# A graph network's x1·adj product made by seven block products in place of eight, from the third batch on

## The chip, the cores and the metric

The kernel runs on one core of one Trainium2 chip. The metric is device time in microseconds of one execution. The kernel before takes 539.05 us (median of three runs, 538.93 to 540.27).

## The reference, cut to what matters

Sixteen batches, each with node features `x` (512 x 256) and its own matrix `adj` (512 x 512), pass through four graph layers and two layer norms, all in float32:

```
num = adj.sum(axis=-1, keepdims=True)
x1 = layernorm(x + (adj @ (x @ W0 + b0)) / num)
a  = relu(adj @ (x1 @ W1) + b1)
b  = relu(adj @ (a @ W2) + b2)
out = layernorm(x1 + adj @ (b @ W3) + b3)
```

## The kernel before, in words

Every batch is cut into T = 4 tiles of 128 nodes and KF = 2 halves of 128 features. To keep float32 precision on TensorE, each operand is held as a pair: `hi`, a copy rounded to float32r, and `lo`, the rest. A product is then three matmuls, hi·hi, hi·lo and lo·hi (`three_passes`, L184 to L188). ScalarE makes each `hi` (`copy_hi`, L487, or a relu, L586), VectorE the matching `lo` by a subtraction (`sub_hi`, L694). For the inputs adj and xT the `lo` comes from GpSimd (L984, L991).

The products of a batch are numbered in the code. p0 is x·W0, its result h; p1 is adj·h, from which the first norm (`norm1`) makes x1; p2 is x1·adj in transposed form, its result g (256 features by 512 nodes); p3 is g·W1 (x2), p4 x2·W2 (s2), p5 s2·adj (x3), p6 x3·W3 (s3), p7 adj·s3, followed by the second norm (`norm2`) and the store.

The main loop overlaps three batches. `step(new)` works at `old` (one batch earlier) and `nxt` (one later). TensorE's queue in a step is p5(old), p2(new), p6(old), p3(new), p7(old), p0(nxt), p4(new), p1(nxt). p2 and p5 use moving tiles of 512 columns, all others 256. One step runs for each of the batches 1 to 14; the last batch has a tail of its own. Each engine executes its own queue in the order written in its `step`, and engines wait for one another by semaphores:

- ScalarE: relu of x3 (two halves, each once to `hi` and once in place in PSUM), g, split of xT(nxt), s3, x2, then `norm2(old)` with a row sum of adj beside each tile, h(nxt), s2(new), `norm1(nxt)` with the split of the batch after next's adj tiles.
- VectorE: the `lo` parts in the same order, `norm2`, h, s2, `norm1`. In `norm2` tile j's order is v2 (L840), then for tile j-1 the reciprocal, then `bn_stats` (L847), the normalization y of tile j-1 (a tensor_scalar, L853), and `bn_aggr` (L859); ScalarE answers each `bn_aggr` with a square root (L607). `norm1` has the same shape (L793 to L817), with the tensor_scalar at L804.
- GpSimd: waits until x1 is fully split (L997), then adj_lo (4 instructions), xT_lo (2), x + b0 (4), x1 + b3 (4).
- SyncE: one queue, in order: adjT of a batch in two halves (waits `adj_split`), xT, x, adj, then the store of an earlier batch, which waits for that batch's last y. The next batch's adjT stands behind that store.

PSUM is eight banks: `bank_a[0:4]` and `bank_b[0:4]`. v1, s3 and v2 use the left half of `bank_b`; x3 and x2 use `bank_a[0:2]`, g uses `bank_a[2:4]`.

Of the kernel before, what the change touches and what calls it, by code (L numbers as in the profile page):

```python
# [10 lines left out]
P = 128  # L11
# [8 lines left out]
def build(nc, xT, x, adjT, adj, w0, w123, b03, b12, out):  # L20
# [8 lines left out]
    with ExitStack() as ctx:  # L29
# [29 lines left out]


# [4 lines left out]
        g_hi, g_lo = pair("g", [P, KF, N])  # L65
        x2_hi, x2_lo = pair("x2", [P, KF, N])
        x3_hi, x3_lo = pair("x3", [P, KF, N])
# [10 lines left out]
        y = sb("y", [P, T, F], F32)  # L78
# [47 lines left out]
        p2_done = sem("p2_done")  # L126
        p3_done = sem("p3_done")
# [43 lines left out]
        def out_of(batch):  # L171

            return v1 if batch is LAST else y
# [19 lines left out]
        xT1_raw, x1_raw = y, v2  # L193
# [19 lines left out]
        def _(sp):  # L213
# [38 lines left out]
            sp.dma_start(out[0], y[:, :, :]).then_inc(stored, DMA)  # L252
            with sp.Fori(3, NB) as i:
                load(i, lambda half: sp.wait_ge(adj_split, (i - 3) * T + (half + 1) * T // 2),
                     lambda: sp.wait_ge(rows_ready, i * T))

                sp.wait_ge(y_ready, (i - 1) * T)
                sp.dma_start(out[i - 2], y[:, :, :]).then_inc(stored, DMA)
            sp.wait_ge(y_ready, (NB - 1) * T)
            sp.dma_start(out[NB - 2], y[:, :, :]).then_inc(stored, DMA)  # L260

            for j in range(T):
                sp.wait_ge(y_ready, (NB - 1) * T + j + 1)
                sp.dma_start(out[NB - 1, :, j, :], out_of(LAST)[:, j, :]).then_inc(stored, DMA)
# [3 lines left out]
        def _(pe):  # L268
# [114 lines left out]
            def p3(new):  # L383

                pe.wait_ge(g_split, at(new, KF, KF))
                for f in range(KF):
                    cols = slice(f * P, (f + 1) * P)

                    for side in (slice(0, N // 2), slice(N // 2, N)):
                        for k in range(KF):  # L390
                            mm = three_passes(pe, bank_x2(new)[f][:, side],
                                              (w_hi[:, 1, k, cols], w_lo[:, 1, k, cols]),
                                              (g_hi[:, k, side], g_lo[:, k, side]), k == 0, k == KF - 1)
# [11 lines left out]
            def p6(old, reader, read):  # L405
# [31 lines left out]
            def step(new):  # L437
                old, nxt = before(new), before(new, -1)
                p5(old)
                p2(new)  # L440
                p6(old, v1_ready, new)
                p3(new)
# [22 lines left out]
            with pe.Fori(0, TURNS - 1) as turn:  # L465
# [7 lines left out]
            p2(LAST)  # L473
            p6(old, v1_ready, LAST)
            p3(LAST)
# [9 lines left out]
        def _(act):  # L485
# [55 lines left out]

            def s3(old):
                hi = s3_last_hi if old is LAST else s3_hi
                for j in range(T):
                    if j == 0 and old is not LAST:
                        act.wait_ge(p6_done, at(old, T, 1))
                        act.activation(s3_half[:, :], bank_b[0][:, F:2 * F], ACT.Copy).then_inc(s3_second_half, 1)
# [21 lines left out]

            def norm1(new, ahead, turns=range(T + 1)):  # L570
# [8 lines left out]

            def g(new, f):  # L580
                act.wait_ge(p2_done, at(new, KF, f + 1))
                copy_hi(g_hi[:, f, :], bank_g(new)[f][:, :]).then_inc(g_hi_ready, 1)

            def relu_split(done, batch, f, bank, bias, hi, ready):
                act.wait_ge(done, at(batch, KF, f + 1))
                act.activation(hi[:, f, :], bank[:, :], ACT.Relu, bias=bias[:, f:f + 1])  # L586

                act.activation(bank[:, :], bank[:, :], ACT.Relu,  # L588
                               bias=bias[:, f:f + 1]).then_inc(ready, 1)

# [6 lines left out]
            def x3(old, f):  # L597
# [3 lines left out]
                relu_split(p5_done, old, f, bank_a[f], b2_col, x3_hi, x3_hi_ready)  # L601

            def norm2(old, tiles=range(T), nxt=None):

                for j in tiles:
# [3 lines left out]
                    if nxt is not None:  # L609
                        row_sum(nxt, j)  # L610

            def step(new, last=False, ahead=True):
                old, nxt = before(new), before(new, -1)
                x3(old, 0)
                x3(old, 1)
                g(new, 0)
# [3 lines left out]
                g(new, 1)  # L620
# [3 lines left out]
                if not last:  # L624
                    norm2(old, nxt=nxt)
                    h(nxt)
                    s2(new)
                    norm1(nxt, before(new, -2) if ahead else None)
# [48 lines left out]
            with act.Fori(0, TURNS - 1) as turn:  # L677
# [6 lines left out]
            x3(LAST, 0)  # L684
            x3(LAST, 1)
            norm2(before(LAST), range(2, 3))
# [5 lines left out]
        def _(dve):  # L692
# [88 lines left out]
            def norm1(new):  # L781

                for j in range(T + 2):
                    a, b, c = j, j - 1, j - 2
                    if a == 0:
# [33 lines left out]
            def g(new, f):  # L819
                dve.wait_ge(g_hi_ready, at(new, KF, f + 1))  # L820
                sub_hi(g_lo[:, f, :], bank_g(new)[f][:, :], g_hi[:, f, :]).then_inc(g_split, 1)
# [9 lines left out]
            def norm2(old, turns=range(T + 1), banks=bank_b):  # L831

                for j in turns:
                    a, b = j, j - 1
                    if a == 0:

                        dve.wait_ge(x1b_ready, at(old, T, T))
                    if a < T:
                        dve.wait_ge(p7_done, at(old, T, a + 1))
                        dve.tensor_tensor(v2[:, a, :], banks[a][:, 0:F], x1b[:, slot(old), a, :],  # L840
# [4 lines left out]
                    if a < T:  # L845
                        dve.wait_ge(v2_ready, at(old, T, a + 1))
                        dve.bn_stats(stats2[:, a, :], v2[:, a, :]).then_inc(stats2_ready, 1)  # L847
                    if b >= 0:
                        if b == 0 and old is not LAST:

                            dve.wait_ge(stored, at(old, DMA, DMA))
                        dve.wait_ge(rstd2_ready, at(old, T, b + 1))
                        dve.tensor_scalar(out_of(old)[:, b, :], v2[:, b, :], moments2[:, b, 0:1], rstd2[:, b:b + 1],  # L853
# [7 lines left out]
            def step(new, last=False):  # L861
                old, nxt = before(new), before(new, -1)
                x3(old, 0)
                x3(old, 1)
                g(new, 0)
                g(new, 1)
# [3 lines left out]
                if not last:  # L870
                    norm2(old)
                    h(nxt)
                    s2(new)
                    norm1(nxt)
# [187 lines left out]
```

## Time and profile before

| | |
|---|---|
| median of three runs | 539.05 us |
| the profiled execution | 539.36 us, span 537.6 us |
| granted TensorE clock | 0.998 of full speed |
| TensorE busy | 530.4 us, 3829 matmuls |
| VectorE busy | 351.2 us (65%) |
| ScalarE busy | 313.6 us (58%) |
| GpSimd busy | 208.3 us (39%) |
| one step of the main loop | 32.7 us |

The span is from the first to the last instruction; about 1.8 us of the execution's own time lies around it. Busy shares are averages over the whole span. Recorded durations of matmuls overlap, because the engine is pipelined: the distance between the starts of two matmuls is what one costs.

### The profile page before, as it was taken

The numbers are of one execution on the slowest core, as the hardware profiler recorded it, in microseconds if no ns is written. First come the engines' busy times: TensorE is split into PE (matmuls) and PEld (weight loads), VectorE is DVE, ScalarE is ACT, GpSimd is POOL, SyncE is SP. The second block draws the span as 40 slices with busy tenths as digits, with TensorE's granted clock in tenths as the row PEclk, the third lists the DMA queues.
The fourth block names the chain that finished last, engine by engine and source line by source line (L and its number), as shares of the span: only waits on it lengthen the run. The fifth ranks groups of instructions, "written<-read, shape, count | busy, mean of one in ns | idle before, by whom it ended". The sixth has DMA issues, their size and how long they took to land.

```text
span 537.6 us, 11046 instructions
## 1 busy us (share of the span) xinstructions
PE 530.4 (99%) x3829; PEld 497.0 (92%) x3829; DVE 351.2 (65%) x1061; ACT 313.6 (58%) x790; POOL 208.3 (39%) x225
## 2 busy tenths in 40 slices
PE   8999999999999999999999999999999999999996
PEld 7899989999899998989999899998999989899896
DVE  4884756747576575766747567475675757667546
ACT  5856566565665556655475665656655566554542
POOL 3749045090541807227081450905418062271100
PEclk9999999999999999999999999999999999999999
DMA  8530430705216060250703407042060612500002
GB/s 322 207 119 1 122 153 1 275 2 177 96 39 234 0 237 37 63 210 0 273 0 99 174 0 273 0 166 107 31 242 0 233 41 62 215 1 39 2 1 78
DMA packets 14566, 58.23 MB, mean 108 GB/s; under 512 B 1744, under 2 KB 2256, under 8 KB 12752
## 3 DMA queue, kind: packets, MB, share of 16 engines
q1 hardware_dynamic: 13824, 55.58, 28.3%
q10 hardware_dynamic: 720, 2.36, 1.2%
q8 instruction: 13, 0.21, 0.2%
q14 instruction: 9, 0.07, 0.0%
HBM read 49.55 MB, written 8.39 MB: 108 GB/s over the span
## 4 chain that ended last, share of the span: by engine, by line
PE 94%; DVE 2%; ACT 1%; issue 1%; DMA 1%; POOL 1%; POOLq 0%; DVEq 0%; SPq 0%
PE bank_a L186 16%; PE bank_a L187 16%; PE bank_a L188 16%; PE bank_b L186 15%; PE bank_b L188 15%; PE bank_b L187 15%; PE bank_b L278 1%; DMA xT_raw<-in_xT 1%; PE bank_b L279 1%; ACT x L565 0%; DVE stats L847 0%; ACT std L607 0%; ACT x_hi L567 0%; PE bank_b L314 0%; POOL w_both L954 0%
## 5 line engine op out<-in xcount | busy, mean ns | idle before, releaser
L984 POOL TENSOR_TENSOR adj_lo<-adj_raw,adj_hi 128x512 fp32r<-128x512 f32 x56 | 70.9, 1297 | 261.7 <-ACT adj_hi L487 261.7
L694 DVE TENSOR_TENSOR x_lo<-bank_a,x_hi 128x512 fp32r<-128x512 f32 x62 | 42.9, 692 | 66.9 <-ACT bank_a L588 66.9
L186 PE MATMUL bank_b<-h_hi,adj_hi 128*128 128x256 f32 (+1 forms) x256 | 71.1, 278 | 0.7 <-issue 0.5
L188 PE MATMUL bank_b<-h_hi,adj_lo 128*128 128x256 f32 (+1 forms) x256 | 70.8, 277 | 0.0
L187 PE MATMUL bank_b<-h_lo,adj_hi 128*128 128x256 f32 (+1 forms) x256 | 70.8, 277 | 0.0
L555 ACT ACTIVATE std<-moments,eps_col 128x1 f32<-128x1 f32 x64 | 18.9, 295 | 84.9 <-DVE moments L817 82.0
L188 PE MATMUL bank_b<-s_hi,adj_lo 128*128 128x256 f32 x232 | 64.1, 276 | 0.0
L186 PE MATMUL bank_b<-s_hi,adj_hi 128*128 128x256 f32 x232 | 64.0, 276 | 0.0
L187 PE MATMUL bank_b<-s_lo,adj_hi 128*128 128x256 f32 x232 | 64.0, 276 | 0.0
L586 ACT ACTIVATE x_hi<-bank_a,b_col 128x512 fp32r<-128x512 f32 x62 | 42.4, 684 | 20.6 <-PE bank_a L188 19.5
L949 POOL TENSOR_TENSOR x1b<-x,b_all 128x256 f32<-128x256 f32 x64 | 46.2, 748 | 17.2 <-DVE x L804 17.2
L186 PE MATMUL bank_a<-adj_hi,s_hi 128*128 128x512 f32 x128 | 50.1, 391 | 0.0
L187 PE MATMUL bank_a<-adj_lo,s_hi 128*128 128x512 f32 x128 | 50.0, 390 | 0.0
L188 PE MATMUL bank_a<-adj_hi,s_lo 128*128 128x512 f32 x128 | 49.8, 389 | 0.0
L607 ACT ACTIVATE std<-moments,eps_col 128x1 f32<-128x1 f32 x64 | 18.9, 295 | 51.9 <-DVE moments L859 51.9
L186 PEld LDWEIGHTS bank_b<-h_hi,adj_hi 128*128 128x128 f32 x256 | 48.1, 188 | 1.0 <-issue 1.0
L187 PEld LDWEIGHTS bank_b<-h_lo,adj_hi 128*128 128x128 f32 x256 | 48.1, 188 | 0.0
L188 PEld LDWEIGHTS bank_b<-h_hi,adj_lo 128*128 128x128 f32 x256 | 48.1, 188 | 0.0
L694 DVE TENSOR_TENSOR g_lo<-bank_a,g_hi 128x512 fp32r<-128x512 f32 x30 | 20.8, 692 | 40.0 <-ACT g_hi L487 40.0
L186 PE MATMUL bank_a<-adj_hi,x_hi 128*128 128x512 f32 x120 | 46.7, 389 | 0.0
L187 PE MATMUL bank_a<-adj_lo,x_hi 128*128 128x512 f32 x120 | 46.7, 389 | 0.0
L188 PE MATMUL bank_a<-adj_hi,x_lo 128*128 128x512 f32 x120 | 46.7, 389 | 0.0
(154 smaller groups left out, 1719.4 us busy)
## 6 DMA issues: line engine op xcount, KB each, us to landing
adj_raw<-in_adjT SPq DMA_DIRECT2D x29, 512.0 KB, 5.4
adj_rows<-in_adj SPq DMA_DIRECT2D x14, 1024.0 KB, 9.2
xT_raw<-in_xT SPq DMA_DIRECT2D x15, 512.0 KB, 6.4
out_y<-y SPq DMA_DIRECT2D x15, 512.0 KB, 2.9
x_raw<-in_x SPq DMA_DIRECT2D x14, 512.0 KB, 7.2
w_raw<-in_w SPq DMA_DIRECT2D x1, 768.0 KB, 13.4
adj_raw<-in_adjT ACTq DMA_DIRECT2D x1, 512.0 KB, 6.1
x_raw<-in_x ACTq DMA_DIRECT2D x1, 512.0 KB, 8.1
```

The source lines that it names most:

```text
L186: pe.matmul(acc, st[0], mv[0], start=start, stop=False)
L187: pe.matmul(acc, st[0], mv[1], start=False, stop=False)
L188: return pe.matmul(acc, st[1], mv[0], start=False, stop=stop)
L278: pe.matmul(bank[j][:, 0:2 * F], hi, w_both[:, n, k, :, :], start=True, stop=False)
L279: mm = pe.matmul(bank[j][:, 0:F], lo, mv[0], start=False, stop=False)
L555: act.activation(std1[:, j:j + 1], moments1[:, j, 1:2], ACT.Sqrt, bias=eps_col[:, :]).then_inc(std1_ready, 1)
L586: act.activation(hi[:, f, :], bank[:, :], ACT.Relu, bias=bias[:, f:f + 1])
L607: act.activation(std2[:, j:j + 1], moments2[:, j, 1:2], ACT.Sqrt, bias=eps_col[:, :]).then_inc(std2_ready, 1)
L694: return dve.tensor_tensor(lo, full, hi.bitcast(F32), ALU.subtract)
L949: pool.tensor_tensor(x1b[:, slot(batch), j, :], x1[:, j, :], b3_all[:, :], ALU.add).then_inc(x1b_ready, 1)
L984: pool.tensor_tensor(adj_lo[:, s, k, :], adj_raw[:, k, :], adj_hi[:, s, k, :].bitcast(F32), ALU.subtract).then_inc(adj_split, 1)
```

## The change

p2 for the batches 2 to 15 is computed by a Winograd-Strassen scheme. x1 is seen as 2 x 2 blocks (two tiles of nodes by 128 features), adj as 2 x 2 blocks (two tiles by 256 columns). Seven products m1 to m7 of such blocks take the place of eight: each is two tiles x three passes = six matmuls of 256 columns, written to half banks of PSUM. Four of the seven need sums of x1 blocks (S1 to S4, VectorE), and four need sums of adj blocks (T1 to T4, GpSimd), and each sum is again split in `hi` (ScalarE) and `lo` (VectorE for S, GpSimd for T). VectorE then combines the products: c11 = m1 + m2, u = m6 + m1, w = m7 + u, v = m5 + u, c21 = m4 + w, c22 = m7 + v, c12 = m3 + v. Batch 1 keeps the old form.

Further edits come with it. ScalarE's g follows the combinations, with both halves after them; `split_xT` moves behind g; `row_sum` of the last tile moves behind h; one `split_adj` tile moves from `norm1` into the next step. GpSimd's step gets four sums T after adj_lo and four T_lo at its end, and starts when all S are split. The store now reads v2, which is normalized in place. VectorE does the last y of `norm2` after h. SyncE's load of adjT waits for the four sums T in place of `adj_split`. x3 shares its buffer with x2, g with h, the sums T live in the buffer of the raw weights, and m1's copy, u, v and w live in `xb`. The first turn of the loop is written out.

```diff
+            def p2_by_seven(new):
...
+                pe.wait_ge(x1_split, at(new, T, 2))
+                product(m1, x1_block(0, low), adj_block(low, left)).then_inc(m1_done, 1)
+                pe.wait_ge(x1_split, at(new, T, T))
+                product(m2, x1_block(0, high), adj_block(high, left)).then_inc(m2_done, 1)
+                pe.wait_ge(T_split, at(new, 4, 4 - 8))
+                pe.wait_ge(S_split, at(new, 4, 1 - 8))
+                product(m7, S_block(S3), T_block(T3))
+                product(m4, x1_block(1, high), T_block(T4))
+                pe.wait_ge(S_split, at(new, 4, 3 - 8))
+                product(m6, S_block(S2), T_block(T2)).then_inc(m6_done, 1)
+                product(m5, S_block(S1), T_block(T1)).then_inc(m5_done, 1)
+                pe.wait_ge(S_split, at(new, 4, 4 - 8))
+                pe.wait_ge(c11_added, at(new, 1, -1))
+                product(m3, S_block(S4), adj_block(high, right)).then_inc(m3_done, 1)
...
             def p6: ready(j):
+                    if by_seven and j > 0:
+                        pe.wait_ge((u_ready, v_ready, m1_copied)[j - 1], at(read, 1, -1))
...
         ScalarE:
             def step(new, last=False, ahead=True, by_seven=True):
                 x3(old, 0)
+                    split_S(new, S1)
+                x3_in_place(0)
+                    split_S(new, S2)
+                    copy_m1(new)
+                    split_S(new, S4)
                 x3(old, 1)
+                x3_in_place(1)
+                        split_adj(nxt, T - 1)
+                    g_by_seven(new)
+                s3_halved(old)
                     split_xT(nxt, 0)
                     split_xT(nxt, 1)
                 s3(old)
                 x2(new, 0)
                 x2(new, 1)
+                    for i in range(4):
+                        split_T(nxt, i)
                     norm2(old, nxt=nxt)
                     h(nxt)
+                    row_sum(nxt, T - 1)
                     s2(new)
+                    norm1_and_S(nxt, before(new, -2) if ahead else None)
...
         VectorE:
             def step(new, last=False, by_seven=True):
+                    sum_S(new, S2)
+                    sum_S(new, S4)
+                    split_S(new, S1)
+                    x3(old, 0)
+                    split_S(new, S2)
+                    add_c11(new)
+                    split_S(new, S4)
+                    x3(old, 1)
+                    add_u(new)
+                    add_w(new)
+                    add_v(new)
+                    add_c21(new)
+                    add_c22(new)
+                    add_c12(new)
+                    g(new, 1, 0)
+                    g(new, 0, 1)
                 s3(old)
                 x2(new, 0)
                 x2(new, 1)
+                    norm2(old, range(0, T))
                     h(nxt)
+                    norm2(old, range(T, T + 1))
                     s2(new)
+                    norm1(nxt, first_sums=not by_seven)
...
         GpSimd:
             def step(new, by_seven=True):
+                    pool.wait_ge(S_split, at(new, 4, 4 - 8))
                 split_adj(nxt)
+                sum_T(nxt)
                 split_xT(nxt)
                 add_b0(nxt)
                 add_b3(new)
+                split_T(nxt)
```

`sum_S(S3)` and `sum_S(S1)` with `split_S(S3)` stand in VectorE's last two turns of `norm1`, the copy of S3 in ScalarE's. `sum_T` is four subtractions of 128x512 elements, `split_T` four more; on ScalarE `split_T` is one 128x512 copy each.

## Rows read from the trace of the kernel before

**Rows 1.** The page: busy times, granted clock by slice, shares of the last chain

```profile
PE 530.4 (99%) x3829; PEld 497.0 (92%) x3829; DVE 351.2 (65%) x1061; ACT 313.6 (58%) x790; POOL 208.3 (39%) x225
PEclk9999999999999999999999999999999999999999
PE 94%; DVE 2%; ACT 1%; issue 1%; DMA 1%; POOL 1%; POOLq 0%; DVEq 0%; SPq 0%
```

**Rows 2.** Timeline, TensorE: start us, duration, instruction; where p2, p6, p7, p0 begin

```profile
205.38 0.39 PE L186 MATMUL bank_a<-adj_hi,x_hi 128*128 128x512 f32 x1
...
210.82 0.40 PE L278 MATMUL bank_b<-w_both,x_hi 128*128 128x512 f32 x1
...
216.27 0.28 PE L186 MATMUL bank_b<-s_hi,adj_hi 128*128 128x256 f32 x1
...
221.71 0.39 PE L278 MATMUL bank_b<-w_both,xT_hi 128*128 128x512 f32 x1
```

**Rows 3.** Timeline, SyncE: store, load, next store; from the page, adjT's time to landing

```profile
224.44 0.36 SPq L258 DMA_DIRECT2D out_y<-y  x1
225.35 0.91 SPq L234 DMA_DIRECT2D adj_raw<-in_adjT  x2
...
257.12 0.36 SPq L258 DMA_DIRECT2D out_y<-y  x1
...
adj_raw<-in_adjT SPq DMA_DIRECT2D x29, 512.0 KB, 5.4
```

**Rows 4.** Timeline, ScalarE, one step; [idle before it <- who released it]

```profile
204.37 0.42 ACT L487 ACTIVATE x_hi<-x 128x256 fp32r<-128x256 f32 x1
204.69 0.62 ACT L487 ACTIVATE adj_hi<-adj_raw 128x512 fp32r<-128x512 f32 x1
205.21 0.67 ACT L586 ACTIVATE x_hi<-bank_a,b_col 128x512 fp32r<-128x512 f32 x1
205.78 0.65 ACT L588 ACTIVATE bank_a<-bank_a,b_col 128x512 f32<-128x512 f32 x1
...
219.55 0.29 ACT L607 ACTIVATE std<-moments,eps_col 128x1 f32<-128x1 f32 x1 [1.84 <-DVE moments L859]
...
224.13 0.36 ACT L531 ACTIVATE h_half<-bank_b 128x256 f32<-128x256 f32 x1
224.99 1.21 ACT L487 ACTIVATE h_hi<-bank_b 128x256 fp32r<-128x256 f32 x4 [0.50 <-DVE bank_b L720]
```

**Rows 5.** Timeline, VectorE, the same step

```profile
217.74 0.69 DVE L694 TENSOR_TENSOR x_lo<-bank_a,x_hi 128x512 fp32r<-128x512 f32 x1 [0.61 <-ACT bank_a L588]
218.35 0.41 DVE L840 TENSOR_TENSOR v<-bank_b,x1b 128x256 f32<-128x256 f32 x1
218.80 0.43 DVE L847 BATCH_NORM_STATS2 stats<-v 128x6 f32<-128x256 f32 x1
...
228.72 0.48 DVE L798 SCALAR_TENSOR_TENSOR v<-bank_b,inv_rows,xb 128x256 f32<-128x256 f32 x1 [0.43 <-PE bank_b L188]
...
236.61 0.42 DVE L804 TENSOR_SCALAR x<-v,moments,rstd 128x256 f32<-128x256 f32 x1
```

**Rows 6.** Timeline, GpSimd in the step: its first, second and last pieces

```profile
205.40 5.06 POOL L984 TENSOR_TENSOR adj_lo<-adj_raw,adj_hi 128x512 fp32r<-128x512 f32 x4 [19.45 <-ACT adj_hi L487]
210.43 2.58 POOL L991 TENSOR_TENSOR xT_lo<-xT_raw,xT_hi 128x512 fp32r<-128x512 f32 x2
...
215.79 2.85 POOL L949 TENSOR_TENSOR x1b<-x,b_all 128x256 f32<-128x256 f32 x4
```

**Rows 7.** Timeline of the start, GpSimd

```profile
32.29 0.72 POOL L949 TENSOR_TENSOR x1b<-x,b_all 128x256 f32<-128x256 f32 x1
```

**Rows 8.** Timeline of the start, VectorE beside it

```profile
27.80 1.81 DVE L694 TENSOR_TENSOR w_both<-w_raw,w_both 128x512 fp32r<-128x512 f32 x1
...
32.32 0.84 DVE L766 TENSOR_SCALAR x<-v,moments,rstd 128x256 f32<-128x256 f32 x1
33.09 0.41 DVE L770 BATCH_NORM_STATS2 stats<-v 128x6 f32<-128x256 f32 x1
```

More of the change, by code:

```diff
@@ L58, in build @@
         s2_hi, s2_lo = pair("s2", [P, T, F])
+        S_hi, S_lo = pair("S", [P, 4, 2, P])
         inv_rows = sb("inv_rows", [P, T], F32)
@@ L64, in build @@
         xT_hi, xT_lo = pair("xT", [P, T, F])
-        g_hi, g_lo = pair("g", [P, KF, N])
+        T_hi, T_lo = pair("T", [P, 4, 2, N // 2])
         x2_hi, x2_lo = pair("x2", [P, KF, N])
-        x3_hi, x3_lo = pair("x3", [P, KF, N])
+        x3_hi, x3_lo = x2_hi, x2_lo
         s3_hi, s3_lo = pair("s3", [P, T, F])
@@ L191, in build, with rows_of, g_of @@
         adj1_raw = adj_rows
-        xT1_raw, x1_raw = y, v2
+        xT1_raw, x1_raw = v2, S_raw.rearrange("p a b c -> p a (b c)")
+        T_raw = w_raw
+        S3, S1, S2, S4 = range(4)
+        T1, T3, T2, T4 = range(4)
+        def rows_of(t, width):
+            return t.rearrange("p a b -> p (a b)")[:, 0:KF * width].rearrange("p (k n) -> p k n", k=KF)
+        def g_of(batch):
+            hi, lo = (s3_hi, s3_lo) if batch is FIRST else (h_hi, h_lo)
+            return rows_of(hi, N), rows_of(lo, N)
+        left, right = slice(0, N // 2), slice(N // 2, N)
+        c11, c12 = bank_a[2][:, left], bank_a[2][:, right]
+        c21, c22 = bank_a[3][:, left], bank_a[3][:, right]
+        m2, m3, m4, m7 = c11, c12, c21, c22
+        m6, m5, m1 = [bank_b[j][:, right] for j in range(1, T)]
+        m1_copy, u, v, w = [xb[:, j, :] for j in range(T)]
         def bank_g(batch):
@@ L464, in _ @@
             pe.wait_ge(w123_split[2], 1)
-            with pe.Fori(0, TURNS - 1) as turn:
+            for r in range(1, RING + 1):
+                step((0, r), by_seven=r > 1)
+            with pe.Fori(1, TURNS - 1) as turn:
                 for r in range(1, RING + 1):
@@ L676, in _ @@
             norm1(second, third, range(2, T + 1))
-            with act.Fori(0, TURNS - 1) as turn:
+            for r in range(1, RING + 1):
+                step((0, r), by_seven=r > 1)
+            with act.Fori(1, TURNS - 1) as turn:
                 for r in range(1, RING + 1):
@@ L913, in _ @@
             norm1_early(second, range(3, T + 2))
-            with dve.Fori(0, TURNS - 1) as turn:
+            for r in range(1, RING + 1):
+                step((0, r), by_seven=r > 1)
+            with dve.Fori(1, TURNS - 1) as turn:
                 for r in range(1, RING + 1):
@@ L1020, in _ @@
                 add_b3(FIRST, range(j, j + 1))
-            with pool.Fori(0, TURNS - 1) as turn:
+            pool.wait_ge(w0_split, 1)
+            pool.wait_ge(w123_split[2], 1)
+            for r in range(1, RING + 1):
+                step((0, r), by_seven=r > 1)
+            with pool.Fori(1, TURNS - 1) as turn:
                 for r in range(1, RING + 1):
```

246 lines of the change are left out of this document (196 added, 50 removed).

## The prediction, made before the changed kernel ran

> **What bounds the kernel now.** I read the page first: TensorE is 99% busy, its clock stands at the upper level (2.4 GHz, granted 9 or more tenths in all slices), and 94% of the last chain is TensorE's [rows 1]. Then its timeline. p2's 24 matmuls of 512 columns run from 205.38 to 210.82, so one costs 5.44/24 = 0.227 us; p7's 48 of 256 columns from 216.27 to 221.71, 0.1133 us each [rows 2]. There is no gap between products: TensorE waits for nothing. A step takes 257.12 - 224.44 = 32.68 us [rows 3]. Last I read the other queues of one step, since the question is how much room they leave.
>
> **What p2 saves.** 42 matmuls of 256 columns x 0.1133 = 4.76 us in place of 5.44: 0.68 us a batch, 14 batches, 9.5 us. The price per column is the same at both widths [rows 2], and p7 too changes its weights at every matmul, so more weight changes cost nothing by themselves. If nothing else were late: 539.36 - 9.5 = 529.8 us by the profiled execution, a step of 32.0.
>
> **The chain of the helpers.** ScalarE and VectorE hand work to each other in a circle: norm1, x3, g, s3, x2, norm2, h, s2, norm1. Now it closes with room only because TensorE feeds it: v1 waits 0.43 us for TensorE at 228.72 [rows 5]. I follow the circle in the changed queues from A, the start of v1 of tile 0, using distances between starts, TensorE taken as ready.
> - A to x1 of tile 3: 236.61 - 228.72 = 7.89 [rows 5]. ScalarE's copy of tile 3 would follow 0.45 later (8.34), but S3's copy stands before it: 8.65 (a 256 copy costs 204.69 - 204.37 = 0.32, [rows 4]).
> - From there ScalarE has no pause: x1, x3 (0.57), S1, x3 in place, S2, m1's copy (0.27), S4, x3, x3 in place. The 256 copies cost 0.31, each relu 205.78 - 205.21 = 0.57 [rows 4]. The last one starts at 11.88, and VectorE follows 0.68 later: 12.56.
> - VectorE: x3_lo 218.35 - 217.74 = 0.61, then u, w, v, c21, c22, c12 at some 0.34 to 0.45 each (a dependent one costs 218.80 - 218.35 = 0.45, [rows 5]). c12 starts at 15.0. ScalarE's two g copies: 15.10 and 15.59, then s3's half 16.08 and the two of xT: 17.39. s3's four copies (as h's, 1.21 for four, [rows 4]) end at 18.56, s3_lo at 19.3.
> - x2's four relus: 2.28, to 20.84. Then four copies of T (0.53 each), the last not before GpSimd's T4. GpSimd starts when S4 is split, 12.4; adj_lo takes 5.06 [rows 6] and the four T, of the same form, as much: 22.5. The T4 copy ends at 23.13, where norm2's first root starts; without T it could start at 22.76.
> - Three tiles of norm2 at 1.25 (219.55 to the fourth root, three turns, and 0.2 to h_half at 224.13 less the row sum that moves away): h_half at 27.1, h_hi at +0.86 = 27.95 [rows 4]. Four copies to 29.04, row sum 0.61, s2's four; VectorE, which has h_lo, the last y and s2_lo in between, reaches v1 of the next batch at 31.84.
>
> So the circle needs 31.84, against TensorE's 32.0. There is one more term: the last y now comes after h, at 30.3, some 2.5 us later in its step than before, and adjT's load stands behind the store in SyncE's queue. It is issued 0.19 + 0.91 later, 31.4, and lands 5.4 after that [rows 3], 36.8; ScalarE wants it at A + 3.70 = 35.54. The wait eats its own pause before the next root (A + 5.24) and 0.16 remains, between 0 and 0.4. Everything is balanced to a few tenths: 32.0.
>
> **What I did not find room for.** GpSimd has 14 instructions a step now and 22 after, some 23.4 us: from A + 12.4 to about A + 36, that is to 4 us into the next norm1. Now it is done at 218.6, before the first y (two turns after v2 at 218.35), and does not start until norm1 is over [rows 6], so no y or x1 of the main loop ever meets it. After, all four y and x1 of tile 0 do. What such a meeting costs the trace shows once: the tensor_scalar of x1 issued at 32.32 took 0.84 us, and what followed it started 0.77 later, where the loop's duration of 0.42 [rows 5] leaves 0.32 to the next; GpSimd's add, begun at 32.29, ended at 33.01 [rows 7, 8]. That looks like waiting for the whole instruction of GpSimd. A subtraction with both inputs in SBUF, of a form that costs 0.69 where it has one in PSUM, took 1.81 in the same stretch [rows 8].
> So a tensor_scalar costs what is left of GpSimd's instruction, less 0.24. For y of tile 0: T4's end releases ScalarE's copy (0.53), the root (0.33 to the reciprocal), 0.08, 0.32: y is issued about 1.32 after T4's end. GpSimd begins its second xT_lo 1.23 after it. y comes just behind it and loses 0.96. y of tiles 1 and 2 meet the adds of 0.71: 0.3 each. The last y meets an add or a T_lo, its place less certain: 0.41, the mean over a 1.26 instruction. x1 of tile 0 falls near the end of T_lo: nothing. Sum 1.96, bounds 0 (below nothing is excluded, a meeting gives nothing back) and 2 x 1.02 + 2 x 0.47 = 3.0. VectorE's other work of that stretch has one input in PSUM, as x_lo and v2 at 217.74 and 218.35 have, which keep 0.69 and 0.41 while GpSimd adds until 218.6 [rows 5, 6]; I cost it at nothing. S's sums and S_lo, with both inputs in SBUF, fall between T_lo's end and GpSimd's start, by its new wait.
>
> The Trainium skill, SBUF — State Buffer, section Who interferes with whom, states this rule: VectorE and GpSimd share a pair of ports, an instruction in the two-port mode (a float32 tensor_scalar from SBUF to SBUF may be in it) takes the pair for its whole length, and the one that comes second is blocked. The row at 32.32 agrees, with 0.84. By the rule the sum is the one above; if it did not hold, the sum ends at the circle of 32.0.
>
> **The sum.** A step of 31.84 + 0.16 + 1.96 = 33.96 against 32.68: +1.28, for 13 steps 16.6; the last batch keeps its 0.68. 539.36 + 16.6 - 0.7 = 555.3 by the profiled execution, 0.3 above the median of the runs: 555.0. TensorE then waits about 2 us a step, first for h_lo (before p1) and v2, then for the splits of x3 and g.
>
> **Rivals.**
> - *The queues just fit* (the other side). The meeting costs next to nothing, and the step is 32.0 to 32.2, with TensorE pausing 0.1 to 0.2 at g (its last split ends at A + 17.0, which is 13.4 us into the step; p3 wants it at 13.3). For it: the circle as worked out. Against: the 0.84. It gives 539.36 - 14 x 0.68 + 13 x 0.1 = 531; 532 with the store's delay. It decides when the meetings cost under 0.7 us a step.
> - *y slips in front.* y of tile 0 is 0.1 us behind the start of xT_lo; a tenth earlier it waits for the instruction before, which is nearly over. Then y costs 0.2 in all, but T_lo ends later into norm1 and x1 of tile 0 pays up to 0.55: a step of 32.8, 13 x 0.1 - 0.7: 540.
> - *All at the worst phase*: 3.0 in place of 1.96 and 0.4 for the load: 35.2, 572.
>
> **Chances.** Forecast 0.50 (its own range 545 to 565), queues just fit 0.31, since one row carries the whole price against it, y in front 0.15, worst phase 0.04. A measurement of this kernel can tell 0.3% from no change, 1.6 us. Faster: 0.31 and a third of 0.15, 0.36. Same: a third of 0.15 and the edge of the forecast's spread, 0.08. Slower: 0.56. The range that holds 8 in 10 reaches down to the case that fits: 531 to 563.
>
> **What would show it.** Right: y of norm2 much longer than 0.40 us, over 1 us for tile 0; a step of 33 to 34.5; TensorE idle before p1 and p3; GpSimd busy from p6 to beyond the next step's start. Wrong: y at 0.40 us beside a busy GpSimd; or a step near 32.0 with v1 again waiting for TensorE. If p2 itself is not 4.76 us, the first term is wrong.

## The result, and the profile after

The changed kernel takes 572.2 us (median; 570.1 to 581.2) against 539.2 (538.9 to 540.3): ratio 1.061, interval 1.059 to 1.063. It is slower, as forecast, but by 33 us and not by 16, above the range (531 to 563). The profiled execution is the slowest of the five, 581.2; where its extra 9 us lie is said below. One execution each of runs 7 and 13, over 1.5% above their others (644.7 and 586.0 us), is left out of their times.

The page of the changed kernel: busy times, granted clock by slice, the last chain, and y's group (its mean was 0.40 us in the kernel before).

```profile
PE 547.2 (94%) x4081; PEld 521.2 (90%) x4081; DVE 457.4 (79%) x1271; ACT 356.2 (61%) x916; POOL 351.4 (61%) x337
PEclk9999799999999999999999999769999999999999
PE 31%; DVE 24%; issue 15%; ACT 13%; POOL 8%; DMA 7%; SPq 1%; DVEq 0%; POOLq 0%
L1065 DVE TENSOR_SCALAR v<-v,moments,rstd 128x256 f32<-128x256 f32 x64 | 65.3, 1020 | 0.6
```

TensorE's share of the last chain fell from 94% to 31% [rows 1]; the 64 instructions y take 1.02 us in the mean. SyncE's stores (the columns as in [rows 3]) give the step:

```profile
206.68 0.36 SPq L299 DMA_DIRECT2D out_y<-v  x1
...
240.91 0.36 SPq L299 DMA_DIRECT2D out_y<-v  x1
```

Of the 13 steps between two stores nine take 33.9 to 34.2 us, where 33.96 was forecast; two take 34.7 and 35.3, and two, at 240.91 and 346.08, 37.0 and 46.6. In one of the ordinary steps VectorE's four y and, in the second fence, GpSimd beside them:

```profile
96.19 1.39 DVE L1065 TENSOR_SCALAR v<-v,moments,rstd 128x256 f32<-128x256 f32 x1
98.44 0.61 DVE L1065 TENSOR_SCALAR v<-v,moments,rstd 128x256 f32<-128x256 f32 x1
99.91 0.61 DVE L1065 TENSOR_SCALAR v<-v,moments,rstd 128x256 f32<-128x256 f32 x1
103.65 0.98 DVE L1065 TENSOR_SCALAR v<-v,moments,rstd 128x256 f32<-128x256 f32 x1
```

```profile
94.86 2.58 POOL L1224 TENSOR_TENSOR xT_lo<-xT_raw,xT_hi 128x512 fp32r<-128x512 f32 x2
97.37 3.00 POOL L1176 TENSOR_TENSOR xb<-x_raw,b_all 128x256 f32<-128x256 f32 x4
100.33 2.90 POOL L1182 TENSOR_TENSOR x1b<-x,b_all 128x256 f32<-128x256 f32 x4
103.18 2.61 POOL L1247 TENSOR_TENSOR T_lo<-w_raw,T_hi 128x512 fp32r<-128x512 f32 x2
```

Over 0.40 they lose 0.99, 0.21, 0.21 and 0.58: 1.99 a step, where 1.96 was forecast. The first y ends at 97.58, as GpSimd's second xT_lo does (97.44). The next two meet adds that start 0.72 apart, and the last a T_lo. So far each y ends 0.15 after the one instruction of GpSimd that it met. Two y of the 64 did not: first VectorE, then GpSimd.

```profile
56.51 7.54 DVE L1065 TENSOR_SCALAR v<-v,moments,rstd 128x256 f32<-128x256 f32 x1
...
377.07 9.38 DVE L1065 TENSOR_SCALAR v<-v,moments,rstd 128x256 f32<-128x256 f32 x1
```

```profile
58.95 4.95 POOL L1247 TENSOR_TENSOR T_lo<-w_raw,T_hi 128x512 fp32r<-128x512 f32 x4
...
381.36 4.93 POOL L1247 TENSOR_TENSOR T_lo<-w_raw,T_hi 128x512 fp32r<-128x512 f32 x4
```

The first ends at 64.05, the second at 386.45; the last T_lo end at 63.90 and 386.29. These y waited out the rest of GpSimd's unbroken run, eight and eleven instructions with the one under way. Two other pauses of some 3 us stand where a turn of the loops ends (VectorE, then TensorE behind it):

```profile
254.88 0.43 DVE L950 TENSOR_TENSOR S_raw<-S_raw,x 128x256 f32<-128x256 f32 x1 [2.96 <-issue]
```

```profile
257.09 0.39 PE L204 MATMUL bank_b<-T_hi,S_hi 128*128 128x256 f32 x1 [2.71 <-DVE S_lo L848]
```

"issue" says that VectorE waited for nothing that the profile shows. The other pause ends at 360.19 and is 3.10 us long. TensorE then stood idle for 2.9 us, and its granted clock fell to 0.50 (the lower level, 1.2 GHz) from 364 to 368. The wait of 9.38 came in the same step, TensorE idle for 7.1 in p0 and the granted clock again at 0.50 from 388 to 392: the step took 46.6 us. Less the pause, which the other turn's end has too, that is 9.5 us over an ordinary step, about what the profiled execution has over the median (9.0). Whether the other executions had such a wait is not known.

TensorE in the changed kernel, where p2, p6, p7 and p0 begin (as [rows 2]):

```profile
216.74 0.28 PE L204 MATMUL bank_b<-adj_hi,x_hi 128*128 128x256 f32 x1
...
222.38 0.40 PE L319 MATMUL bank_b<-w_both,x_hi 128*128 128x512 f32 x1
...
228.04 0.28 PE L204 MATMUL bank_b<-s_hi,adj_hi 128*128 128x256 f32 x1
...
233.69 0.39 PE L319 MATMUL bank_b<-w_both,xT_hi 128*128 128x512 f32 x1
```

p7's 48 products, which the change did not touch, take 233.69 - 228.04 = 5.65 us; before, 5.44 [rows 2]. This row did not decide the time of this kernel (run 13), but what the change can give at most (runs 6, 9 and 14).

### The profile page after: what moved, and what is told of

Read it like the earlier page. It is cut to its first block, busy times and chain, and to the rows that moved or that the text cites. A ratio compares the mean times of both kernels' runs of the same rounds, so it can differ in the third digit from the quotient of the medians.

```text
span 579.4 us, 12001 instructions
## 1 busy us (share of the span) xinstructions
PE 547.2 (94%) x4081; PEld 521.2 (90%) x4081; DVE 457.4 (79%) x1271; ACT 356.2 (61%) x916; POOL 351.4 (61%) x337
## 4 chain that ended last, share of the span: by engine, by line
PE 31%; DVE 24%; issue 15%; ACT 13%; POOL 8%; DMA 7%; SPq 1%; DVEq 0%; POOLq 0%
DMA adj_raw<-in_adjT 7%; PE bank_a L204 6%; PE bank_a L206 6%; PE bank_a L205 6%; PE bank_b L204 4%; PE bank_b L205 4%; PE bank_b L206 4%; POOL w_raw L1235 4%; ACT T_hi L577 4%; POOL adj_lo L1217 3%; DVE stats L1062 2%; DVE h_lo L848 2%; DVE v L1065 2%; ACT std L740 2%; DVE x L1015 2%
## 5 line engine op out<-in xcount | busy, mean ns | idle before, releaser
L204 PE MATMUL bank_b<-h_hi,adj_hi 128*128 128x256 f32 (+1 forms) x256 | 73.0, 285 | 4.4 <-DVE h_lo L848 4.1
L1247 POOL TENSOR_TENSOR T_lo<-w_raw,T_hi 128x512 fp32r<-128x512 f32 x56 | 71.5, 1307 | 0.0
L1065 DVE TENSOR_SCALAR v<-v,moments,rstd 128x256 f32<-128x256 f32 x64 | 65.3, 1020 | 0.6
L1182 POOL TENSOR_TENSOR x1b<-x,b_all 128x256 f32<-128x256 f32 x64 | 46.8, 758 | 4.9 <-DVE x L1015 4.9
L1176 POOL TENSOR_TENSOR xb<-x_raw,b_all 128x256 f32<-128x256 f32 x60 | 44.4, 770 | 0.0
L577 ACT ACTIVATE adj_hi<-adj_raw 128x512 fp32r<-128x512 f32 x60 | 37.5, 626 | 11.0 <-DMA adj_raw<-in_adjT 10.9
```

What stands on the lines that cost most here:

```text
L204: pe.matmul(acc, st[0], mv[0], start=start, stop=False)
L577: return act.activation(dst, src, ACT.Copy)
L1065: dve.tensor_scalar(v2_of(old)[:, b, :], v2_of(old)[:, b, :], moments2[:, b, 0:1], rstd2[:, b:b + 1], ALU.subtract, ALU.mult).then_inc(y_r ...
L1176: pool.tensor_tensor(xb[:, j, :], raw[:, j, :], b0_all[:, :], ALU.add).then_inc(xb_ready, 1)
L1182: pool.tensor_tensor(x1b[:, slot(batch), j, :], x1[:, j, :], b3_all[:, :], ALU.add).then_inc(x1b_ready, 1)
L1247: pool.tensor_tensor(T_lo[:, i, :, :], T_raw[:, i, :, :], T_hi[:, i, :, :].bitcast(F32), ALU.subtract).then_inc(T_split, 1)
```

## The experiments

Ratios are to the kernel before, with their 95% intervals. Theory A: what is lost is lost where y meets GpSimd. Its rival B: something else in the added work is late, and y only stands beside it.

**1. y without the two operands' arithmetic.** It leaves the normalization of y out.

```
-  dve.tensor_scalar(v2[:, b, :], v2[:, b, :], moments2[:, b, 0:1], rstd2[:, b:b + 1], subtract, mult)
+  dve.bn_stats(stats_dummy[:, b, :], v2[:, b, :])
```

> The changed kernel with the y instruction of the second norm (a tensor_scalar from SBUF to SBUF) replaced by a bn_stats of the same input, which takes 0.41 us as y does alone; the normalization of the output is left out. All waits and queues stay. Theory A (y meets GpSimd's instructions and waits for them, and for a whole run of them in the first step): the 1.98 us a step and the 7 us of the first step go, the step falls from 34.0 to 32.0-32.2 us, and the time to about 537, of which 6 us are two pauses of 3 us at the loop's ends. Theory B (the circle of ScalarE and VectorE is simply longer than worked out, whatever GpSimd does): the time stays within 5 us of 572.

557.2 us, 1.032 (1.031 to 1.034): 15 us come back, not 35. The long wait is gone, the first step (by p5's starts) is back from 39.9 to 32.7, and no bn_stats waits. But VectorE is now earlier, and x1 of tile 0, at 0.40 in the changed kernel, meets T_lo (VectorE, GpSimd):

```profile
133.38 1.53 DVE L1016 TENSOR_SCALAR x<-v,moments,rstd 128x256 f32<-128x256 f32 x1
```

```profile
132.15 2.62 POOL L1247 TENSOR_TENSOR T_lo<-w_raw,T_hi 128x512 fp32r<-128x512 f32 x2
```

1.1 us of the 2.0 that y gave back are lost there, up to 1.25 in other steps: the cost moved to the next tensor_scalar. The ordinary step is 33.5.

**2. y with a sum beside it.** The same instruction with an accumulated column, which does not apply the scale to each element (that part is left out).

```
+  ..., subtract, mult, junk[:, b:b + 1])
```

> The changed kernel with y as a tensor_scalar that also writes an accumulator (into a column nobody reads), everything else as it is. Theory A with the mode of the instruction as cause (it takes both ports only in its fast form): y takes 0.5 us beside GpSimd in every step, never over 1 us, no long wait; step 32.2-32.6 us, time 538 to 543. Rival A2 (any VectorE instruction from SBUF to SBUF of this kind waits for GpSimd, in whatever form): y stays at 1.4, 0.6, 0.6, 1.0 us and the time at 572. Theory B: 572 or a little more, with y at 0.5 us.

559.3 us, 1.036 (1.034 to 1.038). This form takes 0.52 to 0.54 us beside GpSimd in every step. So not every instruction of VectorE that reads v2 waits; its form decides. The time missed the 538 to 543 expected, as run 1 missed its 537: here too x1 of tile 0 takes 1.2 to 1.45.

**3. The loops written out** (`for turn in range(1, TURNS - 1)` in place of `Fori(1, TURNS - 1)`, on the four compute engines).

> The changed kernel with the loop over turns written out on all four engines. Theory C (two pauses of 3 us before VectorE's first sum of S, at the jump back to the loop's start): both go, and with them the fall of TensorE's clock that followed the second in the profiled run: time down by 6, to 565-567. Rival: the pause is the fetch of instructions as such and comes elsewhere or more often in a longer program: 570 or more.

567.4 us, 1.052 (1.050 to 1.054): 4.8 us less than the changed kernel, and the pauses of 3 us are gone. The steps stay at 33.9, the wait at 56.79 at 7.54 us. TensorE, where p5 begins in the second step and in the last batch:

```profile
77.06 0.39 PE L204 MATMUL bank_a<-adj_hi,s_hi 128*128 128x512 f32 x1
...
517.97 0.39 PE L204 MATMUL bank_a<-adj_hi,s_hi 128*128 128x512 f32 x1
```

The kernel before has the same kind of loop, and its turns' ends show no such pause. VectorE there, behind a turn's end and in a step without one:

```profile
141.09 0.69 DVE L694 TENSOR_TENSOR x_lo<-bank_a,x_hi 128x512 fp32r<-128x512 f32 x1 [1.22 <-ACT bank_a L588]
...
173.78 0.69 DVE L694 TENSOR_TENSOR x_lo<-bank_a,x_hi 128x512 fp32r<-128x512 f32 x1 [1.22 <-ACT bank_a L588]
```

In both VectorE stands idle for 1.22 us, waiting for ScalarE. A pause of up to 1.2 us could hide there, one of 3 could not. What makes a turn's end of the changed kernel cost that much stays open.

**4. The meeting by itself.** VectorE and GpSimd alone, one instruction of VectorE a trial against a row of GpSimd's adds, issued later from trial to trial.

> A kernel of its own, in which only VectorE and GpSimd work: GpSimd adds in runs of 14 (128x256, 0.71 us apart) or 10 (128x512, 1.26 us apart), and one VectorE instruction is issued after the fourth of them, later by 0.08 us from trial to trial. It computes nothing of the reference. Theory A: a tensor_scalar takes 0.15 us plus what is left of the GpSimd instruction; and, as the two long cases of the changed kernel (issued with 0.39 and 0.20 us left of an instruction) against the short ones (0.46 or more left), those issued in the last 0.4 us or so wait for the end of the whole run, 6 us and more. Rival A3 (the long wait has nothing to do with the moment of issue): no trial waits for a run, or it does at random. The tensor_tensor from SBUF behaves like the tensor_scalar, bn_stats stays at 0.41 throughout, and the tensor_scalar with an accumulator at 0.5 if its form decides.

443.2 us in all. VectorE's rows: against adds of 256 columns, the same five trials later, against adds of 512, and the form with a sum:

```profile
8.45 0.79 DVE L70 TENSOR_SCALAR vc<-va,one 128x256 f32<-128x256 f32 x1 [3.06 <-POOL pc L54]
...
57.44 0.47 DVE L70 TENSOR_SCALAR vc<-va,one 128x256 f32<-128x256 f32 x1
...
108.09 1.33 DVE L70 TENSOR_SCALAR vc<-va,one 128x256 f32<-128x256 f32 x1 [10.42 <-POOL pc L54]
...
376.02 0.52 DVE L72 TENSOR_SCALAR_CACHE_REDUCE vc<-va,one 128x256 f32<-128x256 f32 x1
```

Alone it takes 0.41. Issued 0.065 us later each time, it takes 0.065 less: a wait for the end of GpSimd's instruction, never beyond. A tensor_tensor waits in the same way (0.42 to 0.93), the form with a sum and bn_stats never. No moment of issue gave a long wait, so the moment alone does not make it.

**5. and 6. The same results without a meeting.** x1 and y as a scalar_tensor_tensor whose second operand is the reciprocal root, a column in PSUM read over and over; TensorE gets two waits, so that it does not clear the columns too soon. First with the loops, then with them written out.

```
-  dve.tensor_scalar(y, v2, mean, rstd2[:, b:b + 1], subtract, mult)
+  dve.scalar_tensor_tensor(y, v2, mean, rstd_psum[:, b:b + 1].broadcast_to([P, F]), subtract, mult)
```

> The changed kernel with y and x1 of the main loop's two norms as scalar_tensor_tensor, the reciprocal root read as a broadcast column from a free place in PSUM: the same result by an instruction that has one input in SBUF and one in PSUM, as v1's has, which takes 0.47 us in place of 0.40. TensorE gets two waits that should be satisfied already. Theory A (with y replaced alone, the step was 33.5 us, since x1 of tile 0 then met T_lo and took 1.5 to 1.65 us): no meeting is left in the loop, the step falls to the circle's own 32.0-32.3 plus 8 x 0.07, 32.5 to 32.9 us; time 540 to 545, of which 5 to 6 us are the two pauses at the loop's ends. Theory B (the circle itself is longer): the step stays at 33.3 or more, 550 or more.

> The same with the loop written out on the four engines. The pauses at the loop's ends go (they went in the changed kernel written out, which took 5 us less): 5 us below psum_all, 535 to 540. Rival: with shorter steps the pauses were partly hidden, and it is 2 us or less.

550.3 us, 1.021 (1.019 to 1.022), and written out 541.4, 1.004 (1.002 to 1.005). Against the runs of 572.2 and 567.4 the meetings cost 22 and 26 us. Both times are above what was expected (540 to 545, 535 to 540). Writing out gave 8.9 us in place of 5: the two steps with a turn's end take 35.3 and 37.1. y takes 0.46 to 0.48, beside GpSimd or not:

```profile
221.48 0.47 DVE L1081 SCALAR_TENSOR_TENSOR v<-v,moments,bank_a 128x256 f32<-128x256 f32 x1
```

But a step is 32.66, not the 32.0 that TensorE was to need (written out; five of the 13 take 32.8 to 33.1). At first I laid that to the circle of ScalarE and VectorE. The timeline of TensorE contradicts it (p2, p6, p7, p0, p1 begin):

```profile
206.60 0.28 PE L204 MATMUL bank_b<-adj_hi,x_hi 128*128 128x256 f32 x1
...
211.60 0.40 PE L319 MATMUL bank_b<-w_both,x_hi 128*128 128x512 f32 x1
...
217.26 0.28 PE L204 MATMUL bank_b<-s_hi,adj_hi 128*128 128x256 f32 x1
...
222.91 0.39 PE L319 MATMUL bank_b<-w_both,xT_hi 128*128 128x512 f32 x1
...
228.37 0.28 PE L204 MATMUL bank_b<-h_hi,adj_hi 128*128 128x256 f32 x1
```

No row of that step has idle time. p2 takes 5.00 (42 x 0.119), p6 with p3 5.66 and p7 5.65, that is 0.1177 a product; from p0 on it is 0.1133 again (5.46 for p0 with p4; before, 5.45). The clock is granted in full throughout.

**7. GpSimd's new work alone.** The kernel before, with four sums and four subtractions a step on GpSimd and the load of adjT behind them.

> The kernel before with GpSimd's new work alone: the four sums T and four instructions in the place of T_lo (T less itself, so that ScalarE has nothing to do with it), at the changed kernel's places in GpSimd's queue; the eight products and every other queue stay, the sums are not used. Theory A: y of the loop takes 0.6 to 1.4 us where it took 0.40, x1 of the first tiles may too; of 1 to 3 us a step about 0.4 has room, so the step is 33.2 to 34.5 and the time 546 to 565, more if y waits for a whole run of GpSimd. Theory B (GpSimd's work is harmless, the sums on the other engines cost): 539 to 541.

610.3 us, 1.132 (1.128 to 1.136), more than the whole change. The first y of two steps:

```profile
95.37 7.44 DVE L857 TENSOR_SCALAR y<-v,moments,rstd 128x256 f32<-128x256 f32 x1
...
216.83 0.65 DVE L857 TENSOR_SCALAR y<-v,moments,rstd 128x256 f32<-128x256 f32 x1
```

In 9 of 14 steps the first y of a step takes 6.7 to 7.5 us, in 5 it takes 0.65 to 0.82. A step with the long wait takes 39.7 to 40.8 us, one without it 33.4 to 34.4 (theory A's range was 33.2 to 34.5). The long wait is thus no accident of one step; it needs neither S nor the seven products. Theory A stands and theory B falls. Six of the long ones and four of the short ones begin 0.23 to 0.27 us into the same add of GpSimd, so the place does not decide.

**8. A run without a pause.** As 4, with bn_stats ahead of an in-place tensor_scalar, against eight adds and four subtractions in a row.

> A kernel of its own, nothing of the reference: GpSimd in runs as behind xT_lo (eight adds of 128x256, four subtractions of 128x512 into float32r), with and without satisfied waits ahead of each; VectorE issues bn_stats and right behind it an in-place tensor_scalar, later by 0.065 us from trial to trial. The first probe showed no wait beyond the instruction under way at any moment. If the long wait of 7.5 us comes from this order of instructions, some trials take 5 us or more; if not, all take 0.4 to 0.8, and the long wait needs something that is only in the whole kernel.

237.5 us in all; 0.40 to 0.90 in every trial, never a long wait. What makes VectorE wait for the rest of the run in the kernels stays open.

**9. p2 of the kernel before in halves.** 48 products of 256 columns in place of 24 of 512.

```
+  for side in (slice(0, N // 2), slice(N // 2, N)):
       for k in range(T):
-          three_passes(bank[f][:, :], x1[:, k, cols], adj[:, s, k, :])
+          three_passes(bank[f][:, side], x1[:, k, cols], adj[:, s, k, side])
```

> The kernel before, with its p2 alone written in products of 256 columns in place of 512 (48 in place of 24, the same columns of work; no S, no T, no new wait). It is to tell where TensorE's slower pace behind the seven products comes from: in the kernel before 256-column products stand 0.1133 us apart everywhere; in the changed kernel and in the one with the PSUM forms they stand 0.1177 to 0.1183 apart from p2's first product to the end of p7 (136 products, 0.60 us a batch), though no wait is seen there. Theory F (the form: a p2 of 256-column products has the slower pace and passes it on to p6, p3 and p7): p2 takes 5.65 in place of 5.44, the 94 products behind it 0.42 more, a batch 33.3, the whole 547 to 549. Theory W (the pace goes down where TensorE's queue meets a wait that is fulfilled just in time, and stays down): the pace stays at 0.1133, the whole within 0.3% of 539.3.

550.4 us, 1.019 (1.018 to 1.021). TensorE at p2, p6, p7, p0:

```profile
209.85 0.28 PE L186 MATMUL bank_a<-adj_hi,x_hi 128*128 128x256 f32 x1
...
215.60 0.40 PE L278 MATMUL bank_b<-w_both,x_hi 128*128 128x512 f32 x1
...
221.26 0.28 PE L186 MATMUL bank_b<-s_hi,adj_hi 128*128 128x256 f32 x1
...
226.91 0.39 PE L278 MATMUL bank_b<-w_both,xT_hi 128*128 128x512 f32 x1
```

p2 takes 5.75 in place of 5.44, p6 to p7 11.31 in place of 10.89 [rows 2]. Theory F: the narrower products alone do it, with no S, T or new wait; the time is a little above its 547 to 549.

**10. p6's first product issued four times**, in the kernel of 6.

> The fully unrolled kernel with the PSUM forms (541.4), in which p6's first product of 512 columns is issued four times over (the first three results are overwritten by the next, 13 batches with three added products of 0.227 us, 0.68 us a batch). Theory Q (at the lower pace TensorE's weight loads or its queue have lost their lead, and columns in surplus give it back): behind the four the 94 products of p6, p3 and p7 go at 0.1133, which gives back 0.41 of the 0.68: a batch 32.9, the whole 541.4 + 14 x 0.27 = 545. Theory S (the pace is set by something else, such as the data or the engines beside it): 0.1177 stays, a batch 33.3, the whole 550 to 551.

547.4 us, 1.014 (1.012 to 1.016). In 13 of the 14 batches with seven products the ones behind are at 0.1133 (p7's first and p0's first):

```profile
219.63 0.28 PE L204 MATMUL bank_b<-s_hi,adj_hi 128*128 128x256 f32 x1
...
225.07 0.39 PE L320 MATMUL bank_b<-w_both,xT_hi 128*128 128x512 f32 x1
```

p7 5.44. Most steps are 32.93, as expected, some 33.1 to 33.5; hence 547.4 and not 545. In the first step, whose p2 has the old form and comes at 0.1133, the four products do the opposite: p7 takes 5.65 behind them. The spacing is a state that can be set from outside.

**11. Earlier helpers**, in the kernel of 6: the copy of T4 behind s2, x1 of tiles 1 to 3 a tensor_scalar again.

> The fully unrolled kernel with the PSUM forms, with the helpers made earlier: ScalarE's copy of the fourth T sum stands behind s2's copies in place of before norm2's first root (0.52 us less in front of the first root, of which the root waits 0.26), and x1 of tiles 1 to 3, which never met GpSimd, is a tensor_scalar again (0.41 in place of 0.47, three times). Theory W (the pace of 0.1177 comes of p2's waits for x1's residuals, which are fulfilled 0.14 us ahead of the product that needs them): with 0.3 to 0.45 us more in hand the pace is 0.1133 to 0.114 for much of p2, p6, p3 and p7, a batch takes 32.0 to 32.3 and the whole is 532 to 537, faster than the kernel before. Theory F (the pace belongs to the seven products themselves): a batch stays at 32.66, as TensorE has no idle time in it to lose; the whole within 0.3% of 541.4.

540.5 us, 1.0015 (1.0006 to 1.0024). The step stays at 32.66 and the spacing at 0.1177: theory W falls, and with it the circle as the bound.

**12. and 13. Two 512-column products in a row** at the head of p6 and p0, in the kernel of 11 and in the changed kernel.

```
   for j == 0:   # was: k = 0 as 512 columns, its lo, then three products of 256 for k = 1
+  for k in range(KF): pe.matmul(bank[0][:, 0:2 * F], hi(k), w_both[:, n, k, :, :])
+  for k in range(KF): pe.matmul(bank[0][:, 0:F], lo(k), w_hi[:, n, k, :])
```

> psum_early, with the first tile of p6 and of p0 made by two products of 512 columns in a row and then two of 256, where there were one of 512 and four of 256: the same columns, the same bank halves, one instruction less each. Theory Q (512-column products in a row give TensorE's front end back its lead): the 94 products behind it go at 0.1133 in place of 0.1177, a batch takes 32.66 - 0.41 = 32.25, the whole 540.5 - 14 x 0.41 = 534.7, faster than the kernel before (539.5). If two do not suffice (psum_again had four, and one does nothing in p6): 0.1177 stays and the whole is 540.5, within 0.2%.

> The changed kernel (572.2) with the same regrouping of p6's and p0's first tile and nothing else: the loops, the tensor_scalars and their waits are as in the changed kernel. Theory H (VectorE's and ScalarE's circle alone sets a batch of 33.96, TensorE has time to spare): the pace behind p6 rises to 0.1133, TensorE waits longer in p0 and at p2, and the whole stays at 570 to 573. Theory T (the helpers in their turn wait for p7's tiles, so TensorE's stretch from p6 to p7 is part of the same circle): a batch loses up to 0.41, the whole is 566 to 568.

early_wide: 540.0 us, 1.0005 (0.9996 to 1.0014), a miss. p6 to p7 went to 0.1133, but p0 to p1, so far at 0.1133, went to 0.1177. after_wide: 575.1 us, 1.067 (1.065 to 1.069), above both expectations; eight of its 13 steps are 33.9 to 34.3, the two with a turn's end 38.4 and 39.0 (one such step of the changed kernel took 37.0). TensorE's quicker stretch buys nothing in the changed kernel, whose ordinary step stays where it was: there the other engines set it (theory H's side).

**14. and 15. The pair at the head of p6 alone**, in the kernel of 11 and in the kernel before.

> psum_early with the pair of 512-column products at the head of p6 alone; p0's head is as it was, with one. The theory that the spacing is a state that TensorE carries on, and that the pair at p6's head leaves it at 0.1133 as in early_wide, while one product at p0's head leaves it there, as in the kernel before and in psum_again: p6, p3 and p7 0.41 a batch less than in psum_early, p0, p3 and p1 unchanged at 0.1133; a batch 32.66 - 0.41 = 32.25, the whole 540.5 - 14 x 0.41 = 534.7, faster than the kernel before (539.5). If the slower spacing comes back in p0 whatever stands there: a batch 32.65, the whole 540.

> The kernel before with the pair of 512-column products at the head of p6 (one instruction less, the same columns). Theory L (512-column products give back a lead): the spacing is 0.1133 ahead of it and stays so, the whole within 0.2% of 539.5. Theory Z (the pair switches between two states, whichever it finds): 0.1177 for the 92 products behind it, 0.41 more a batch, the whole 539.5 + 14 x 0.41 = 545.2.

early_wide_p6: 536.4 us, ratio 0.995 (0.994 to 0.997): with the seven products, half a per cent faster than the kernel before, little but clear of the interval. TensorE and two stores:

```profile
204.38 0.28 PE L204 MATMUL bank_b<-adj_hi,x_hi 128*128 128x256 f32 x1
...
209.36 0.40 PE L316 MATMUL bank_b<-w_both,x_hi 128*128 128x512 f32 x1
...
214.82 0.28 PE L204 MATMUL bank_b<-s_hi,adj_hi 128*128 128x256 f32 x1
...
220.26 0.39 PE L325 MATMUL bank_b<-w_both,xT_hi 128*128 128x512 f32 x1
```

```profile
225.74 0.36 SPq L299 DMA_DIRECT2D out_y<-v  x1
...
257.98 0.35 SPq L299 DMA_DIRECT2D out_y<-v  x1
```

p2 4.98, p6 to p7 10.90, a step of 32.24 as expected. The whole is 1.7 above the 534.7 expected: the first step, whose p2 has the old form, takes 33.5 by p5's starts (32.7 in run 11), since there the pair brings the larger spacing. The same edit makes the kernel before slower, 552.0 us, 1.023 (1.022 to 1.025):

```profile
221.35 0.28 PE L186 MATMUL bank_b<-s_hi,adj_hi 128*128 128x256 f32 x1
...
227.00 0.40 PE L285 MATMUL bank_b<-w_both,xT_hi 128*128 128x512 f32 x1
...
232.66 0.28 PE L186 MATMUL bank_b<-h_hi,adj_hi 128*128 128x256 f32 x1
...
238.31 0.40 PE L186 MATMUL bank_a<-adj_hi,s_hi 128*128 128x512 f32 x1
```

p7 5.65 and p1 5.65: the pair changed the good spacing into the bad one, and p0's single product did not change it back, twice the price that I expected. Theory L falls; "the pair switches" (Z) fits the steps without a pause in all four kernels that have it (not every step of after_wide, whose waits blur the spacing), but what a single 512-column product does differs from kernel to kernel (at p0 it mends the spacing in 11 of 13 steps of run 6, the other two being two of its five longer ones; here in none).

## Why the prediction was right and wrong

- *p2 saves 0.68 us a batch*: wrong. The step that failed is "The price per column is the same at both widths", with what follows from it, "so more weight changes cost nothing by themselves". The row of p7 showed 256-column products at 0.1133 behind a p2 of 512-column ones, and I took it for a price everywhere. A p2 of such products runs at 0.119 and leaves 0.1177 behind it: 0.44 saved in p2, 0.42 lost in p6, p3 and p7, together 0.02 (run 9 shows the cause, run 6 the size). So p2 was not 4.76 but 4.98 to 5.00 where TensorE waits for nothing, by the prediction's own sign a wrong first term. Rival "the queues just fit" at 531 could not have come true: without meetings and loop pauses the change gives 541.4. In the changed kernel itself this decides nothing, since TensorE is not what it waits for (run 13).
- *The circle of 31.84 + 0.16*: not contradicted. With the forms of run 14 it closes within 32.24, as that step has no wait of TensorE. Its exact length no run shows. In run 1 the ordinary step fell by some 0.5, where the losses of y and x1 together fell by 0.75 to 0.9, so the step does not follow their sum to the tenth.
- *A meeting costs what is left of GpSimd's instruction*: right for the ordinary step, in place and size, and with it the step, 33.9 to 34.2 against 33.96. The first y lost 0.99 (0.96 forecast). That the sum fits so well (1.99 against 1.96) is in part luck: y of tiles 1 and 2 lost 0.21 each and not 0.3, the last 0.58 and not 0.41. The Trainium skill, SBUF — State Buffer, section Who interferes with whom, gives the shared ports to whoever issues first for that whole instruction and blocks the other; the probe of run 4 agrees (0.79 down to 0.39), and the rows at 56.51 and 377.07, with 7.54 and 9.38, go beyond that one instruction.
- *Bound of 3.0 a step*: this is the step that failed for the time. It took one instruction of GpSimd as the most that a y can lose, 1.02; the first y of the first step lost 7.14, to the end of GpSimd's whole run. In the unrolled kernel that step takes, from p5 to p5, 77.06 - 36.28 = 40.8 us, where the kernel before has 32.7: 8.1 more, with TensorE idle for 5.3 in p0 and its granted clock at 0.53, near the lower level, from 66 to 70. In runs 1, 2, 5 and 6, where y does not wait, the same step takes 32.7.
- *13 steps at +1.28, 16.6*: right. From 77.06 to 517.97 it is 440.9, where the kernel before takes 424.9 (69.17 to 494.09): 16.0.
- *The last batch keeps its 0.68*: wrong, another step that failed. From its p5 (517.97) to the end of the span it takes 46.8 in place of 43.5, 3.3 more. Its p2 takes 8.62 in place of 5.44, 1.86 of it a wait for a `lo` of x1 at 526.17, and the granted clock is 0.65 from 526 to 530. Without meetings (run 6) that p2 still takes 6.74. Why the helpers are late there I did not follow up.
- *Nothing for the loops*: wrong by omission. Two turns' ends cost 4.8 us (run 3). The rows at 141.09 and 173.78 show that the kernel before did not merely hide them.
- *x1 of tile 0 costs nothing*: right only while y was late. Run 1 shows 1.1 us there when y is not.
- *All at the worst phase, 572*: that this rival's time was measured is a coincidence. Its step of 35.2 is not what the ordinary steps take.

In the unrolled kernel p5 first begins 0.2 earlier than before (36.28 against 36.48). Together -0.2 + 8.1 + 16.0 + 3.3 + 4.8 = 32.0, against 33.0 measured; the last 1.0 is not accounted for. The direction and the mechanism of the ordinary step were right. What put the time outside the range are three terms that I had at nothing or below: the long wait (8.1), the ends of the loops' turns (4.8) and the last batch (3.3 in place of -0.7). The measured time is 9.2 above the range; none of the three alone accounts for that.

## What to carry to other kernels

Before work is moved to GpSimd, list the tensor_scalar and tensor_tensor instructions of VectorE from SBUF to SBUF that will run beside it, and give them a form that does not meet it (with the reciprocal root read from PSUM, 0.47 in place of 0.41): moving or speeding up one of them hands the wait to the next. A duration from one place of a trace is a price for that place only: compare a stretch that the change does not touch, such as p7 here, before and after, even where no idle time is shown. List first and last steps by themselves: a single first step and the last batch held a third of this loss. Look at the ends of a hardware loop's turns after a change, even if they cost nothing before: the same kind of loop showed no pause of over 1.2 us in the kernel before and pauses of 3 in the changed one.

## What the runs showed of the hardware

- VectorE's tensor_scalar beside GpSimd waits to the end of GpSimd's instruction (it takes 0.39 to 1.33 us in the probe of run 4, up to 1.66 in run 1), and in whole kernels at times to the end of its whole run: 6.7 to 9.4 us, in 9 of 14 steps of run 7, in 2 of 14 of the profiled changed kernel, and in none of the trials of runs 4 and 8. The cause is open.
- A tensor_tensor with both inputs in SBUF waits in the same way (0.42 to 0.93 in run 4).
- bn_stats (0.41 to 0.43), the tensor_scalar with an accumulated column (0.52) and a scalar_tensor_tensor with a PSUM operand (0.46 to 0.48) never waited.
- TensorE's products of 256 columns with a weight load each stand 0.1133 or 0.1177 to 0.120 us apart at the same granted clock, and a whole stretch of some 94 (in run 15 from p6 to p1's end, some 190) keeps one of the two. A p2 of 256-column products brings the larger one; a pair of 512-column products in a row switched it in both directions, at no cost of its own. What rule selects it I cannot say.
- The end of a turn of a hardware loop cost VectorE 2.4 to 3.7 us in the five kernels with seven products that keep the loops (runs 1, 2, 5 and 13 and the changed kernel), and nothing with the loops written out. In the kernel before no pause of over 1.2 us is to be seen there. The cause is open.
- TensorE's granted clock was at the lower level, 0.50, for 4 us behind an idle time of 2.9 us, and again behind one of 7.1 us (changed kernel, 364 to 368 and 388 to 392); from 372 to 380 it was at 1.00.
